# Attention 1's first end: between the last exponentials of self-attention, or at the head of the pipeline behind them

## The reference

```python
x = layernorm(x + self_attention(x))                # 16 heads of 16, no mask, 512 keys
x = layernorm(x + cross_attention(x, ctx_1024))     # 16 heads of 16, 64 context rows a batch
x = layernorm(x + mixture_of_experts(x))            # 8 experts, 256 -> 1024 -> 256, gelu, top 2
```

## Time and profile before

| | us |
|---|---|
| timed runs: median of 3 (lowest, highest) | 845.76 (845.61, 847.36) |
| the profiled execution's own time | 842.24 |
| its span | 840.2 |
| TensorE matmul busy | 718.2 |
| TensorE weight loads busy | 465.7 |
| DVE busy | 329.5 |
| ACT busy | 287.2 |
| POOL busy | 220.0 |

### The profile page before, as it was taken

One profiled execution on the slowest core, in us unless ns is written; L12 is line 12 of the kernel. 1 busy time (PEld: TensorE's weight loads), 2 busy tenths in 40 slices (PEclk: granted clock), 3 DMA queues, 4 the chain that ended last, 5 costly groups with the idle time before them and its releaser, 6 DMA issues.

```text
span 840.2 us, 11562 instructions
## 1 busy us (share of the span) xinstructions
PE 718.2 (85%) x3963; PEld 465.7 (55%) x3964; DVE 329.5 (39%) x742; ACT 287.2 (34%) x525; POOL 220.0 (26%) x278
## 2 busy tenths in 40 slices
PE   6899999999998678888979630799999999999970
PEld 3322333322224353647544520799999999999970
DVE  3687776788864360726444430000000000000004
ACT  2246656666764315251433220111111111111112
POOL 2201111111145201010140353133333333333322
PEclk9869999999999899998999655899999999999995
DMA  5974032434341400001030943466665656666506
GB/s 157 185 175 82 5 89 64 77 90 102 58 128 43 151 0 1 1 1 50 1 51 1 226 125 79 148 187 182 172 167 166 172 179 184 179 182 182 166 12 200
DMA packets 58908, 92.80 MB, mean 110 GB/s; under 512 B 13841, under 2 KB 45298, under 8 KB 57331
## 3 DMA queue, kind: packets, MB, share of 16 engines
q1 hardware_dynamic: 50355, 83.86, 36.4%
q0 software_dynamic: 8512, 8.44, 6.2%
HBM read 75.94 MB, written 17.86 MB: 112 GB/s over the span
## 4 chain that ended last, share of the span: by engine, by line
PE 73%; DVE 10%; ACT 5%; DMA 5%; issue 3%; POOL 2%; SPq 1%; POOLq 0%; DVEq 0%; ACTq 0%
PE ps L1705 17%; PE ps L1716 16%; PE ps L1432 7%; PE ps L1423 7%; PE ps L1357 6%; PE ps L1461 3%; DVE nmx L999 3%; PE ps L1375 2%; PE ps L1544 2%; POOL metas L740 2%; ACT probs L828 2%; PE ps L1582 1%; PE ps L1444 1%; PE ps L1572 1%; PE ps L1575 1%
## 5 line engine op out<-in xcount | busy, mean ns | idle before, releaser
L828 ACT ACTIVATE probs<-ps 128x512 f32<-128x512 f32 x256 | 136.0, 603 | 102.7 <-PE ps L1423 102.0
L999 DVE TENSOR_REDUCE nmx<-ps 128x1 f32<-128x512 f32 x256 | 159.8, 681 | 15.7 <-PE ps L1357 15.2
L1705 PEld LDWEIGHTS ps<-xtT,w1c 128*128 128x128 f32 x1248 | 147.3, 194 | 4.3 <-issue 2.4
L1705 PE MATMUL ps<-xtT,w1c 128*128 128x128 f32 x1248 | 147.7, 277 | 1.8 <-ACT xtT L952 1.8
L1716 PE MATMUL ps<-wexp,hidT 128*128 x624 | 141.0, 379 | 0.0
L1319 DVE TENSOR_SCALAR yw<-ps,mt 128x256 f32<-128x256 f32 x39 | 18.9, 484 | 290.5 <-PE ps L1716 290.5
L1716 PEld LDWEIGHTS ps<-wexp,hidT 128*128 128x128 f32 x624 | 115.6, 190 | 14.2
L958 ACT ACTIVATE hidT<-ps 128x1024 f32<-128x1024 f32 x39 | 40.0, 1024 | 229.9 <-PE ps L1705 229.9
L781 POOL DMA_INDIRECT acc<-yw,mt x39 | 61.9, 1587 | 171.9 <-DVE yw L1319 171.9
L1357 PE MATMUL ps<-kst,qst 96*128 96x512 bf16 x256 | 99.2, 409 | 4.9 <-DVE nmx L999 3.3
L1423 PE MATMUL ps<-qst,kst 99*128 99x512 bf16 x256 | 93.9, 390 | 1.1 <-ACT probs L828 0.7
(11 more groups left out here) (192 smaller groups left out, 773.1 us busy)
## 6 DMA issues: line engine op xcount, KB each, us to landing
w1c<-in_w1T SPq DMA_DIRECT2D x39, 1024.0 KB, 5.6
wexp<-in_w2T SPq DMA_DIRECT2D x8, 1024.0 KB, 9.7
kst<-scrk SPq DMA_DIRECT2D x48, 128.0 KB, 7.0
qst<-scrq SPq DMA_DIRECT2D x8, 384.0 KB, 4.8
xTb<-in_xT SPq DMA_DIRECT2D x4, 512.0 KB, 7.6
qst<-scrq SPq DMA_DIRECT2D x8, 256.0 KB, 5.4
xr<-in_x SPq DMA_DIRECT2D x4, 512.0 KB, 5.2
x2d<-xr SPq DMA_DIRECT2D x4, 512.0 KB, 6.0
```

What stands on the lines that cost most here:

```text
L828: act.activation(probs[n % 8][:, :], ps[:, 4 + n % 3, :], ACT.Exp).then_inc(s_exp, 1)
L999: dve.tensor_reduce(nmx[w % 2][:, k:k + 1], ps[:, ring_bank("max", w, k), :], AX.X, ALU.max, negate=True).then_inc(s_mfree, 1)
L1705: mm = pe.matmul(ps[:, 2 * (j % 2) + f // 4, f % 4 * P:(f % 4 + 1) * P], w1c[j % 2][:, k * FF + f * P:k * FF + (f + 1) * P], xtT[j % 2][:, ...
```

## The change

The end of attention 1 of batch 0 is taken out of unit 15 on TensorE, ACT and DVE, and stands in stage 0 as those of the other batches stand in theirs. DVE's two `k2_high_blocks`, which stood among its steps of that end, follow directly on `context_k`. The two waits that stood ahead of the first `end_step` (`s_v2`, `s_k2t`) stand ahead of the stages now, beside those for the key blocks.

```diff
 # ACT
-        FIRST_O2 = {9: 0, 11: 1, 13: 2, 15: 3}
...
-                if u == NUN - 1 and n in FIRST_O2:
-                    copy_o2(0, 0, FIRST_O2[n])
...
-            if e1 is not None and n > 0:
+            if e1 is not None:
                 for t in range(QT):
                     copy_o2(0, e1, t)
 # DVE
             if u == NUN - 1:
                 context_k()
-                first_end()
+                for m in range(KD):
+                    k2_high_blocks(m)
...
-        def first_end():
-            norm_o(0, 0, 0)
-            norm_o(0, 0, 1)
-            k2_high_blocks(0)
-            for t in range(2):
-                norm_o(0, 0, 2 + t)
-                add_residual(0, 0, t)
-            k2_high_blocks(1)
-            for t in range(2, QT):
-                add_residual(0, 0, t)
...
-            if e1 is not None and n > 0:
+            if e1 is not None:
                 norm_o(0, e1, 0)
...
 # TensorE
-        FIRST_END = {5: 0, 7: 1, 9: 2, 11: 3, 13: 4, 15: 5}
...
-                    if u == NUN - 1 and HG * kt + h in FIRST_END:
-                        if FIRST_END[HG * kt + h] == 0:
-                            pe.wait_ge(s_v2, 1)
-                            pe.wait_ge(s_k2t, KD)
-                        end_step(0, 0, FIRST_END[HG * kt + h])
...
         pe.wait_ge(s_fill, FILLED)
+        pe.wait_ge(s_v2, 1)
+        pe.wait_ge(s_k2t, KD)
         pe.wait_ge(s_k2h, KD)
         pe.wait_ge(s_k2l, KD)
         pe.wait_ge(s_v2bd, 2)
...
             def e1_step(step):
-                if e1 is not None and n > 0:
+                if e1 is not None:
                     end_step(0, e1, step)
```

## The result

The changed kernel took 856.40 us in the median of its first four executions (856.33 to 864.65), against 846.56 of the kernel before beside it; the ratio is 1.0136, 95% interval 1.0071 to 1.0200. Timed again for the experiments, it took 857.63 (six executions, 854.82 to 862.10), ratio 1.0106, 1.0054 to 1.0158. Forecast were 854.2 and, over 845.76, a ratio of 1.0100. The direction is right; the loss is 9 to 11.5 us by the two ratios and was put at 8.4. The profiled execution took 856.34 us with a span of 854.3, which is 14.1 above that of before.

What follows compares the result with a forecast made beforehand. Everything after hangs on the query projection behind the first normalise. Unit -10.6, block wait +5.1, exposed end +15.4 - 2.0 were taken as +7.8; with +0.6 for the clock, +8.4 on 845.76 gives 854.2 us, range 849.8 to 857.4.

Steps and rivals of the forecast that it cites:

- step 3: The end alone at the head of the pipeline, first transposes to normalise: 15.4 us, its first half at half clock.
- Step 1: Last unit of self-attention without the end: finishes at about 272.1 instead of 282.74, at most 10.6 us of gain.
- Step 2: Before stage 0 TensorE waits for the key blocks of DVE and POOL, the last ending at 277.2: +5.1 us.
- The reading of the four durations: DVE's and POOL's key-block builds do not run side by side; 11.76 us go one after the other from about 265.5.
- Rival B: DVE's earlier tiles do not delay POOL's: TensorE starts the end at 275.0, 2.2 us sooner, 852.0; chance 0.18.
- The bound for a full clock: The end alone with all of it at full clock: 2.0 us less, so 13.4 us.
- Rival C: TensorE's clock stays up or comes up at once in the end: 2.0 us less, 852.2; chance 0.12.
- D: Clock stays down through the end: 2.0 us more there, 0.8 more in the query projection, 857.0; chance 0.13.
- Step 4: Normalise to query projection: same code, clock may be lower, +0.6 us, between 0 and +2.0.
- Behind the seam: Later stages: same work in the same order, shifted; half-clock stretches change by up to 1.7 us either way.
- rival A: The forecast itself, 854.2 us, with its own range of 852.5 to 856; chance 0.46.
- E: Not slower: blocks done at 275.0, clock never falls in the seam; +1.0 us remains, 846.8; chance 0.07.

Runs made afterwards that it cites:

- blocks_late: Changed kernel with TensorE's and ACT's key-block waits behind stage 0 and DVE's two tiles behind its part of the end; 850.25 us, ratio 1.0021.
- waits_late: Changed kernel with only TensorE's and ACT's key-block waits moved behind stage 0, DVE's tiles left where the change put them; 849.52 us, ratio 1.0013.
- blocks_norm: As blocks_late, but DVE starts its two tiles only after POOL's rstd and shift; 848.05 us, ratio 1.0007 to the kernel before.
- before_hot: Kernel before with added bf16 matmuls in all the gaps where TensorE waits, results untouched; 838.00 us, ratio 0.9870.
- before_warm: Kernel before with 15 added matmuls behind the last PV, in the gap ahead of the first normalise; 849.08 us, ratio 0.9981.

## Why the prediction was right, and where it was not

The mechanism of the seam was right. The step that failed is the one that followed the sum through the later stages: "I expect a shift to change them by up to 1.7 us either way." It entered the sum as nothing, and the runs showed 3.8 us there in one profile of the changed kernel and 5.5 in the other. The term of the sum that was mis-sized is that of step 3, the end alone: 15.4 us forecast, 16.37 and 15.50 measured.

**Step 1, unit 15.** Right. Forecast 10.6 us of gain and an end at 272.1; measured 10.76 (22.46 less 11.70), and 272.83, which is 271.99 after the 0.84 us by which everything ran later.

**Step 2, the wait for the blocks.** Right in mechanism and size. Forecast 277.2 for the last block; measured 277.73, less 0.84: 276.9, and the first transpose at 278.10, less 0.84: 277.26. The wait is 5.27 us, forecast 5.1. The reading of the four durations (the builds do not run side by side) is shown by the profile after, by 7.20 us for POOL's pair alone, and by the rstd of 2.93 us in blocks_late. Rival B is out. That the wait was the heart of the loss is shown by waits_late, which takes back 7.9 us by the ratios and moves nothing but the waits. blocks_late and blocks_norm, which move DVE's tiles as well, take back 7.2 and 8.4; none of the three puts the end back. I treated DVE's queue and the shared path as one with the wait; they are a second obstacle, of 1.3 us behind the first and 2.9 us where DVE's tiles meet POOL's rstd.

**Step 3, the end alone.** The term of 15.4 us measured 16.37 (278.10 to 294.47), 1.0 more. The mis-sized part is the time at half clock: 7.3 us in the row that I took it from, 9.30 here. In the second profile of the changed kernel the end took 15.50 us (278.98 to 294.48), as forecast. There the clock rose ahead of the fourth turn and the output projection behind it. First that profile, then the first one:

```profile
286.46 0.60 PE L1430 MATMUL ps<-identf,oT 128*128 128x128 f32 x4
287.01 1.10 PE L1447 MATMUL ps<-wo_s,o 128*128 128x256 f32 x4
...
285.88 1.06 PE L1430 MATMUL ps<-identf,oT 128*128 128x128 f32 x4
286.73 1.37 PE L1447 MATMUL ps<-wo_s,o 128*128 128x256 f32 x4
```

So a forecast of this term is good to 1 us and no better; that the second came out as forecast is no merit of the sum. The bound for a full clock was 13.4; blocks_norm, at 0.97, took 13.03, so the bound was 0.4 too high. Rival C, the clock up all through the end, did not come; D, down all through, neither.

**Step 4, from normalise to the first cross-attention matmul.** Near: +0.6 forecast between 0 and +2.0, +0.53 measured in the first profile (14.20 against 13.67), -0.1 in the second (13.57).

**Behind the seam.** This is the step that failed. The seam's own sum of 8.4 came out at 9.4 and 7.9 in two profiles. But the rest of the pipeline is 3.8 and 5.5 us longer in them than in the profile of before, more than the 1.7 allowed, with the granted clock at 0.89 and 0.88 against 0.91. A shift of the work is not needed for it: over nine profiles without the fillers that rest took 202.8 to 213.9 us, and in the three kernels with all gaps filled 200.5 to 201.2. What was wrong is the size of the clock's play in the stages, which I had put at 1.7 us without a row for it. For the profiled execution the sum said 850.6 and 856.34 was measured, 5.7 more: 0.8 ahead of the seam, 1.0 in it and 3.9 behind it.

The median, 856.40, lies in the range of 849.8 to 857.4, which reaches 4.4 us below the forecast and 3.2 above it, and 0.4 above rival A's own range. That it fell into the wide range is partly luck: single executions of the changed kernel went from 854.8 to 864.7, and the range took in the steps' bounds and left out that the medians are of few, scattered executions. By the medians of 70 and 10 executions the difference is 9.05, 0.65 above the forecast; the first ratio's interval ends at 17 us. I also said that a measurement of this kernel tells 0.2% from no change; with intervals of 0.3 to 0.65% on each side, it does not.

**The rivals.** E, not slower by a clock that never falls, needed the blocks at 275.0, and is out by step 2.

What stays open: why the clock falls at one gap in one execution and not in the next. The executions differ in it with the same instructions, and I did not find what sets it. Open too is why before_hot's gain, 1.3%, has the size that it has: all its fillers went in together, so what each gap is worth was not measured.

## What to carry to other kernels

When a step moves past a wait that used to be over, look up when the awaited work really ends and what else of the same queues the edit brings forward: here the wait for key blocks cost 5.3 us at a place where the end could have started at once. Large elementwise instructions of VectorE and GpSimd with inputs in SBUF hold each other up, here 128x2048 with two inputs in SBUF, so a small GpSimd operation on the critical path must not meet a large VectorE one (1.04 us became 2.93). In a stretch with many small waits of TensorE, added matmuls in the waits are worth a try, in all of them at once: that gave 1.3%, and one gap filled gave nothing that could be told. And a single profile of such a kernel is a poor base for a sum: the stages behind the change varied by 11 us between profiles.

## What the runs showed of the hardware

The spread of one kernel's executions is TensorE's clock: over 70 executions of the kernel before, 842.8 to 854.5 us went with mean granted clocks of 0.933 to 0.916. With the gaps filled, at 0.961 to 0.965, six executions lay within 4.5 us.

DVE and POOL alternate on their 128x2048 multiplications with two SBUF inputs: pairs that take 4.49 us (DVE alone, blocks_norm) and 7.20 us (POOL alone, blocks_late) end 11.4 us after the first start when issued together (266.35 to 277.73). The Trainium skill's page "SBUF — State Buffer", section "SBUF: two separate sides", calls it an exclusive lock held for a whole instruction. The runs agree for the large tiles. For instructions of 128x4 on POOL they agree in one direction: in blocks_late, where DVE's two tiles ran from 282.70 to 284.98 and on to 287.18, POOL's rstd ended at 285.89 and its shift at 287.25, each only behind a DVE tile. DVE's second tile, with the rstd beside it, took 2.28 us all the same, as alone, so no hold by the small instruction is seen.

Filling one gap need not keep the clock up: in the profile of before_warm the first fall left the query projection and came 1.1 us into the cross-attention behind it.
